# Node updates moved into the edge loop of a two-layer graph transformer

## The reference

```python
for l in range(L):                                   # L = 2
    xn = layernorm(x, ln1_g[l], ln1_b[l])
    xp = xn + xn @ Wpos[l] + bpos[l] + deg * Wdeg[l] + bdeg[l]
    q, k, v = (xp @ W[l] + b[l] for each of the three)
    att = clip(sum_over_head_dim(q[dst] * k[src]) / scale, -50, 50)
    alpha = exp(att) / segment_sum(exp(att), dst)    # softmax per destination
    aggr = segment_sum(v[src] * alpha, dst)
    x = x + aggr @ Wo[l] + bo[l]
    h = gelu(layernorm(x, ln2_g[l], ln2_b[l]) @ W1[l] + b1[l])
    x = x + h @ W2[l] + b2[l]
out = layernorm(x_input + x)
```

## Time and profile before

| | us |
|---|---|
| median of 3 runs | 2277.98 (2273.77 to 2279.02) |
| the profiled execution | 2278.56 |
| its span | 2276.8 |
| busy: PE / DVE / ACT / POOL | 1387.2 / 1400.0 / 778.1 / 1545.3 |
| granted TensorE clock, mean | 0.792 of full speed |

### The profile page before, as it was taken

The page is one execution under the profiler, slowest core; times in us unless marked ns, Lnnn a source line. Parts: engine busy times, 40 slices in busy tenths (PEclk is TensorE's granted clock), DMA queues, the critical chain, the costliest instruction groups (busy, mean ns, idle before and its releaser), DMA issues.

```text
span 2276.8 us, 43094 instructions
## 1 busy us (share of the span) xinstructions
PE 1387.2 (61%) x11435; PEld 1300.2 (57%) x11436; DVE 1400.0 (61%) x2221; ACT 778.1 (34%) x1355; POOL 1545.3 (68%) x1644
## 2 busy tenths in 40 slices
PE   6655565566556666666884545556565665666577
PEld 5545555555556556655764545555555665665567
DVE  8885555656655665666557556556556656656664
ACT  3242223323323333332573222233233333333336
POOL 1577777777777777777117777777777777777731
PEclk9877777777877788888896777777778778888779
DMA  3355545555545545543025554555555455455501
GB/s 85 123 164 161 155 156 160 159 152 160 160 151 160 160 153 158 161 155 114 1 66 169 162 160 154 157 161 155 156 160 159 153 160 160 151 160 160 168 22 29
DMA packets 120614, 322.76 MB, mean 142 GB/s; under 512 B 30847, under 2 KB 43300, under 8 KB 120554
## 3 DMA queue, kind: packets, MB, share of 16 engines
q0 software_dynamic: 75072, 205.10, 29.5%
q1 hardware_dynamic: 44644, 115.35, 16.3%
q10 hardware_dynamic: 838, 1.60, 0.3%
HBM read 313.78 MB, written 8.15 MB: 141 GB/s over the span
## 4 chain that ended last, share of the span: by engine, by line
POOL 60%; issue 21%; PE 8%; DVE 6%; DMA 2%; DVEq 1%; ACT 0%; ACTq 0%; POOLq 0%
POOL kv L470 60%; PE ps L1127 2%; PE ps L1133 2%; DVE q_parts L695 2%; DMA kv<-kv_tab,src_idx 1%; PE ps L1049 1%; PE ps L1080 1%; DVE prod L846 1%; DMA x<-in_x 1%; DVE msg L868 1%; DVEq L316 1%; DVE stats L651 0%; PE ps L1043 0%; PE ps L1119 0%; DVE qkv L754 0%
## 5 line engine op out<-in xcount | busy, mean ns | idle before, releaser
L470 POOL DMA_INDIRECT kv<-kv_tab,src_idx x1564 | 1482.9, 948 | 533.9 <-issue 473.4
L1080 PE MATMUL ps<-msg,hot 128*128 128x136 f32 x3904 | 767.7, 375 | 775.1 <-DVE msg L868 650.7
L1080 PEld LDWEIGHTS ps<-msg,hot 128*128 128x128 f32 x3904 | 712.8, 273 | 813.0 <-issue 813.0
L846 DVE TENSOR_TENSOR prod<-kv,ps 128x1024 f32<-128x1024 f32 x196 | 239.3, 1221 | 637.2 <-DMA kv<-kv_tab,src_idx 635.1
L1066 PE MATMUL ps<-q_parts,hotT 128*128 x5856 | 428.2, 238 | 47.9 <-issue 47.6
L1066 PEld LDWEIGHTS ps<-q_parts,hotT 128*128 x5856 | 410.9, 109 | 65.1 <-issue 51.9
L589 ACT ACTIVATE msg<-att 128x64 f32<-128x64 f32 x196 | 50.2, 256 | 1095.6 <-DVE att L859 1091.7
L827 DVE SCALAR_TENSOR_TENSOR hot<-dst_col,neg_base,ps 128x1024 f32<-128x1024 f32 x244 | 312.0, 1279 | 95.9 <-issue 94.7
L582 ACT ACTIVATE dist<-dst_rows,neg_node 128x1024 bf16<-128x1024 int32 x244 | 280.1, 1148 | 185.2 <-issue 171.5
L585 ACT ACTIVATE hotT<-dist 128x1024 bf16 x244 | 257.8, 1057 | 46.8 <-ACT dist L582 45.5
L849 DVE TENSOR_REDUCE dots<-prod 128x64 f32<-128x1024 f32 x196 | 239.1, 1220 | 6.7
(11 more groups left out here) (160 smaller groups left out, 738.3 us busy)
## 6 DMA issues: line engine op xcount, KB each, us to landing
dst_rows<-in_dst SPq DMA_DIRECT2D x194, 512.0 KB, 3.9
kv<-kv_tab,src_idx POOLq DMA_INDIRECT x1564
kv_tab<-qkv SPq DMA_DIRECT2D x6, 768.0 KB, 3.7
out<-x SPq DMA_DIRECT2D x4, 320.0 KB
kv_tab<-qkv SPq DMA_DIRECT2D x2, 512.0 KB, 3.2
kv_tab<-qkv SPq DMA_DIRECT2D x2, 384.0 KB, 3.3
dst_rows<-in_dst SPq DMA_DIRECT2D x2, 336.0 KB, 3.8
hot<-in_L_gnn_W SPq DMA_DIRECT2D x2, 256.0 KB
```

The lines of the kernel that those rows point to most:

```text
L470: pool.indirect_dma_start(kv[:, u, c, :], None, kv_tab[l][:, :], bass.IndirectOffsetOnAxis(ap=src_idx[:, c, at(g)], axis=0)).then_inc(kv_i ...
L846: nc.vector.tensor_tensor(prod[:, :].rearrange("p (c d) -> p c d", d=D), kv[:, u, :, 0:D], qd[u % 2].rearrange("p (c d) -> p c d", d=D), A ...
L1080: last = MM(agg[:, bass.ds(pr % 2, 1), :], hot[:, u % 2, c, :], msg[:, u % 2, c, :], start=(c == 0), stop=(c == GC - 1))
```

## The change

Three things change together.

1. From group 48 on, every two groups have a **slot** in which one tile's node update runs, from the share-out to the next layer's row or the output row. There are 24 slots (groups 48 to 95). Slot n takes tile `slot_tab[n]`; the table is made on the chip from the destinations (`slot_words_out`) so that a tile's turn comes only when all of its edges are in; where that is not yet so, a tile is done once more. With the given edges the slots do tiles 0 to 21, two of them (14 and 18) twice, and tiles 22, 23 and 24 are left for a tail behind the last group. The pieces of one slot stand at fixed places: in the even group transpose and multiply with Wo, in the odd one the addition, the first norm and the feed-forward net, in the next even one its addition and the second norm, in the next odd one the next layer's row. Each norm is done by itself: bn_stats, bn_aggr, then `Ln` and `Exp` on ACT for the inverse root. ACT loads Gelu's table and then that of `Ln`/`Exp` in every slot.
2. `qd` and `agg` are single, and the slots use the banks: the q product of group g+1 waits for `prod_done` of g (before: of g-1), and each sum for the evacuation of the one before; the evacuation now stands behind the one-hot image in the same group.
3. Biases bo and b2 become one-row matmuls, POOL does no arithmetic any more, each tile has its own store, the whole-layer node stage is gone.

```diff
+                def inverse_root(n, s, which, moments, log, scale):
+                    act.wait_ge(moments, n + 1)
+                    nc.scalar.activation(spot[:, s, which, 8:9], spot[:, s, which, 7:8], ACT.Ln, bias=eps_col[:, :]).then_inc(log, 1)
+                    act.wait_ge(log, n + 1)
+                    nc.scalar.activation(spot[:, s, which, 9:10], spot[:, s, which, 8:9], ACT.Exp, scale=-0.5).then_inc(scale, 1)
...
+                def odd_group(word, d, g, u, r, n, slot):
+                    scale_x2(slot, 0)
+                    weights(u, g)
+                    copy_z1T(slot, 0, in_slot)
+                    gelu(slot, 0, in_slot)
+                    log_and_exp()
+                    if not isinstance(g, int) or g + 2 < NG:
+                        one_hots(word, d + 2, r, n)
+
+                def even_group(word, d, g, u, r, n, slot, first=False, last=False):
+                    weights(u, g)
+                    if not first:
+                        scale_x3(slot - 1, 0)
+                        copy_z2T(slot - 1, 0, in_slot)
+                    if not last:
+                        copy_agT(slot, 0, in_slot)
+                    if not isinstance(g, int) or g + 2 < NG:
+                        one_hots(word, d + 2, r, n)
...
+                def moments(n, s, which, source, summed, stats_done, moments_done):
+                    settle(dve)
+                    dve.wait_ge(summed, n + 1)
+                    nc.vector.bn_stats(spot[:, s, which, 0:6], source).then_inc(stats_done, 1)
+                    settle(dve)
+                    dve.wait_ge(stats_done, n + 1)
+                    nc.vector.bn_aggr(spot[:, s, which, 6:8], spot[:, s, which, 0:6]).then_inc(moments_done, 1)
...
+                    if odd:
+                        if not closing:
+                            current = slot_tile(dve, slot)
+                        if not opening:
+                            next_row(slot_tile(dve, slot - 1), slot - 1, 0, in_slot)
+                        if not closing:
+                            add_attention(current, slot, 0, in_slot)
...
-                    before_last, its_shift = word(d - 2)
-                    if not first:
-                        evacuate(before_last, its_shift)
...
+                    if odd and not closing:
+                        normalise_x2(slot, 0)
+                    if even and not opening:
+                        add_ffn(passed, slot - 1, 0, in_slot)
...
                     one_hot(u, g, tile_of(dve, a, shift))
+                    if not opened:
+                        evacuate(a, last_shift)
...
+                    if even:
+                        if not opening:
+                            normalise_x3(passed, slot - 1, 0)
+                        if not closing:
+                            dve.wait_ge(evac_done[l], a + 2)
+                            share_out(current, slot, 0)
...
-                    if not (isinstance(g, int) and g < 2):
-                        pe.wait_ge(prod_done[l], g - 1)
+                    if not (isinstance(g, int) and g == 0):
+                        pe.wait_ge(prod_done[l], g)
...
+                    if odd:
+                        transpose_z1(slot, 0, in_slot)
+                        hidden(slot, 0, in_slot)
                     pe.wait_ge(msg_done[l], g + 1)
                     sum_pair(u, word(d - 1)[0])
+                    if odd:
+                        project_ffn(slot, 0, in_slot)
+                    if even:
+                        if not opening:
+                            transpose_z2(slot - 1, 0, in_slot)
+                        if not closing:
+                            transpose_ag(slot, 0, in_slot)
+                        if not opening:
+                            project_next(slot - 1, 0, in_slot)
+                        if not closing:
+                            project_out(slot, 0, in_slot)
```

More of the change, by code:

```diff
@@ new lines, in _ @@
+                for n in range(NSLOT - 2, NSLOT):
+                    ready(n + 1)
+                    stored(n)
+                    store(slot_tile(sp, n), 0)
+                start = tail_start(sp)
+                with sp.If(start < NT - TAIL):
+                    with sp.Fori(start, NT - TAIL) as t:
+                        n = early_number(sp, t)
+                        ready(n + 1)
+                        stored(n)
+                        store(t, 0)
+                n = tail_number(sp)
@@ L426, in _ @@
+                stored(n)
+                for f in range(TAIL):
+                    t = NT - TAIL + f
+                    ready(n + f + 1)
+                    store(t, f, N - t * P if t == NT - 1 else P)
+                if l == L - 1:
+                    stored(n + TAIL)
         @block.gpsimd
@@ L629, in _ @@
[L629 to L637 removed]
+                        plain_group(word, u, TURN * i + u, u, (u + 2) % ROWS, TURN // ROWS * i + (u + 2) // ROWS)
@@ L951, in _ @@
+                for t, m, f in tail:
+                    next_row(t, m, f, in_tail[f], before=n)
+                if l < L - 1:
+                    dve.wait_ge(next_done, n + TAIL)
+                    dve.sem_inc(layer_done, 1)
         @block.tensor
@@ L1086, in sum_further, with pe_group @@
                             sum_pair(u, pr)
-                def pe_group(u, g, word, d, more=True):
+                def pe_group(u, g, word, d, more=True, slot=None, opening=False, closing=False):
+                    odd = slot is not None and u % 2 == 1 and not closing
+                    even = slot is not None and u % 2 == 0
                     if more:
@@ L1135, in _ @@
-                pipelined(pe, (0, transposed(2 * l + 1)), (1, hidden), (3, project_ffn))
+                start = tail_start(pe)
+                with pe.If(start < NT - TAIL):
+                    with pe.Fori(start, NT - TAIL) as t:
+                        n = early_number(pe, t)
+                        for part in (transpose_ag, project_out, transpose_z1, hidden, project_ffn, transpose_z2, project_next):
+                            part(n, 0, in_slot)
+                n = tail_number(pe)
@@ L1138 @@
+                for part in (transpose_ag, project_out, transpose_z1, hidden, project_ffn, transpose_z2, project_next):
+                    for f in range(TAIL):
+                        part(n + f, f, in_tail[f])
 _WEIGHTS = ["Wq", "bq", "Wk", "bk", "Wv", "bv", "Wo", "bo", "Wpos", "bpos", "Wdeg", "bdeg",
```

643 lines of the change are left out of this document (371 added, 272 removed).

## The result

The changed kernel takes **2413.16 us** (2411.51 to 2415.79, 4 runs), the kernel before beside it 2276.19 us (2273.77 to 2279.02, 4 runs): ratio 1.0602, 95% interval 1.0584 to 1.0621. The profiled execution spans 2410.0 us against 2276.8. Forecast were 2262 us and a range of 2165 to 2345; the result lies above the range, and it is slower than the kernel before where faster was forecast.

What follows compares the result with a forecast made beforehand. POOL's gathers were taken to bound the kernel, with POOL standing still between stages. Profiled 2278.56 + 4.5 (start) - 79.8 - 63.7 (tails) + 1.4 (last groups) + 68 + 53 (slots) = 2262 us; range 2165 to 2345.

Steps and rivals of the forecast that it cites:

- The tails: Behind each layer's last group, three tiles replace the whole-layer node stage: -79.8 us in layer 0, -63.7 in layer 1.
- Groups 0 to 47 keep POOL's pace: Edge stage before the slots: groups stay at the gathers' pace, 10.0 us each, so no change.
- The single `qd` costs nothing: Groups 0 to 47: q product (1.50 us) hides behind DVE's reducing and clipping; uncovered, 1.5 us would fit the spare 4.
- Mean slot 22.6 (22.0 in layer 1): Groups 48 to 95: 24 slots take 542 us against 480 in layer 0, 528 in layer 1; +68 and +53 net.
- A: Slot whose two groups have no second tile, odd multiplication to next odd one, layer 0: 19.7 us, 6 slots.
- B: Slot with a second tile in the odd group, layer 0: 22.8 us, 7 slots.
- C: Slot with a second tile in the even group, layer 0: 24 us (22.5 to 25), 11 slots.
- In the slots PE idles 2.5 at most: Argument against the lower clock in the slots: slow sums follow 4 us of idling; behind 2.42 a sum took 2.12.
- The clock rival: PE at its lower clock in the slots: 1.5 us more per slot, 72 in all, 2334 us; chance 0.28.
- The drain rival: Each table load in the slots costs 2.66 us, about 2.2 per slot on the path: +104, 2366 us; chance 0.03.
- bn_aggr, Ln and Exp: Slot norms' one-column steps without a row: bn_aggr at least 0.2 us, Ln and Exp nothing; above, 0.5 each.
- What would show it: Gathers evenly paced to about group 60, then waiting some 120 us less twice 20; odd multiplications 20 to 24 apart.

Runs made afterwards that it cites:

- g3: The change with ScalarE's one-hot rows earlier in even groups and VectorE's next row and attention sum, z1 later in odd groups: 2296.67 us, ratio 1.0093.
- g4: The change with relu for gelu and no table loads in the slots, leaving the gelu out of the computation: 2390.45 us, ratio 1.05.
- i1: g3 with slot table behind q rows, second tile ahead of next row and attention, exp/ln table load ahead of layer 1's fold: 2271.51 us, ratio 0.9984.
- g1: The change with ScalarE's one-hot rows ahead of its copies of z2T and agT in even groups: 2428.12 us, ratio 1.0659.
- h1: g3 with gelu's table load ahead of z1's copy in odd groups and the slot table's chain behind the q rows: 2288.6 us, ratio 1.0049.

## Why the prediction was wrong

- *The tails:* right. -74.2 and -61.7 against -79.1 and -63.0. Three tiles in one go take 27.4 us in layer 0, not 23.6. In layer 1 the sum is wrong as it stands: 20.5 less 2.2 plus 0.9 are 19.2 to the last norm, not 18.0, and with the 5.1 behind it 24.3, near the 24.5 measured.
- *Groups 0 to 47 keep POOL's pace:* right, 418.3 us for 44 groups against 418.6; the single `qd` and the second tile's evacuation cost nothing there.
- *"The single `qd` costs nothing, since its product (1.50) runs while DVE reduces and clips":* this was said of groups 0 to 47, and it doesn't carry over to the slots. There TensorE waited 53 and 48 us per layer for prod, 3.0 each time. In g3 that wait is all but gone, with the single `qd` in place.
- *Mean slot 22.6 (22.0 in layer 1):* **this is the step that failed**: it is 25.5 and 25.1. Kinds in layer 0, forecast, change, g3: A 19.7, 22.9, 19.8; B 22.8, 28.2, 25.7; C 24, 25.2, 23.6. I followed each slot as one path from odd prod to odd prod at full clock and took every input from another queue as ready in time. With the two orders of g3, which take the worst waits out, A and C come to the numbers forecast; as the change orders them, ScalarE's copy of z2T and VectorE's next row close a ring. B is still 2.9 above its forecast in g3: its second tile's sum stands behind the q products on TensorE, and in g3's seven slots of this kind VectorE's evacuation, with msg behind it, waited 1.5 to 5.0 us for it. No run moves that sum or the evacuation, so this cause isn't shown.
- *"In the slots PE idles 2.5 at most":* wrong. It idled up to 3.6 us in layer 0's slots and 4.1 in layer 1's, and 2.96 ahead of many q products (888.86), which then took 2.03 and more, where 1.50 was taken.
- *The clock rival (0.3 us a slot decides, 2334):* the direction was right, and in part the reason. A q product took 2.3 us where 1.50 was taken, a sum 2.5 on the average where 2.12 was. But a sum is cheaper there than in the kernel before (3.0), and of the 261 us that both layers' second halves gained, g3 takes back 113 without a change to one matmul.
- *The drain rival (2366):* a table load took 1.28 us and the next activation started 0.01 us behind it (894.86, 896.15), near the 0.02 of the earlier trace rows. Without any load in the slots g4 gained 0.5 us per slot. The Trainium skill (ScalarE: Activation LUTs, What ACT_TABLE_LOAD costs) gives a drain of about 1.38 us on top of each load that switches the set; no row here shows it.
- *bn_aggr, Ln and Exp:* 0.18, 0.28 and 0.20 us, inside the bounds but for bn_aggr, 0.02 under its lower one.
- *What would show it:* POOL's first wait in the slots came at 719.86, about group 60, as was said. Its waits for msg sum to 120 us in layer 0 and 108 in layer 1, 228 in all; said were some 120 in all less 40. The odd prods lay 20.4 to 29.5 apart in layer 0, not 20 to 24.

By its size the slot's price is nearly the whole miss: 24 slots by 2.9 us are 70 us in layer 0, by 3.1 us 74 in layer 1, and groups 44 to 97 are 70 above the forecast in each. These are 140 of 151 us; the start (4.5) and the tails (6) are most of the rest. g3 takes 113 of the 140 back by order alone. After one more reordering (i1) the two stretches are 66.7 and 57.7 us above the kernel before, where 68 and 53 were forecast. That is in part luck: kind B is still 3.0 us dearer there than forecast, and C 1.6 cheaper.

What stays open: what of B's 25.7 us in g3 is the clock and what the order; whether the single `qd` and `agg`, and the evacuation ahead of msg, are what closes the ring, since every run keeps these parts of the change; whether other orders bring the slots to 20.0; and on the two other chips the slow transfers, and why the orders give nothing there.

## What to carry to other kernels

When work is woven into a pipeline of in-order queues, don't add up its path: for each wait that is added, list what stands behind it on that engine and whether one of these feeds, over the other engines, the thing waited for. Where such a ring closes, removing one wait hands its time to the next and may show nothing, so edit both places before giving a theory up. Work that waits for another engine belongs behind what others wait for: here nearly the same instructions took 2272 to 2428 us by their order.

## What was not expected of the hardware

- On two other chips the kernel before took 3272 and 3278 us, 44% more, with groups at 15.0 us in place of 9.5 (groups 0 to 44) and the landing of transfers as the wait; the order of variants turned round there (both orders: 1.047 against 1.0377; on chips like the first 1.0093 against 1.0602).
- On chips like the first, TensorE's granted clock fell from 1.0 to 0.5 around a single idle stretch near the start, and each product of the fold behind it then took 1.65 us instead of 0.91. Behind 4.40 us of idling it was so in all five profiles (the change, g1 to g4), behind 1.65 to 1.67 in four of five (not in h1), behind 1.25 in neither of two (the kernel before). That the idling alone decides it isn't shown, since 1.66 and 1.67 came out differently.
